# Expert rows of six tiles gathered as quarter rows and turned by VectorE, in a mixture-of-experts layer

## The chip, the cores and the metric

The kernel runs on one core of a Trainium2 chip. The metric is the device time of one execution in microseconds (us); lower is better. The times below are of three runs, and one further execution was recorded by the hardware profiler. The core's engines work side by side and meet at semaphores: TensorE (PE; its weight loads are PEld), VectorE (DVE), ScalarE (ACT), GpSimd (POOL) and SyncE (SP), the last two issuing the DMAs.

## The reference

An attention block and a mixture-of-experts block, each behind a layer norm and with a residual:

```
x: (2, 512, 512) f32
x = x + attention(layernorm(x))            # 32 heads of 16
t = layernorm(x)                           # 1024 tokens x 512
p = softmax(t @ gate_w.T)                  # 8 experts
top_vals, top_idx = top_k(p, 2); top_vals /= sum(top_vals)
h1, h3 = t @ w1[e].T, t @ w3[e].T          # (512 -> 800) for each expert e
y[e] = (silu(h1) * h3) @ w2[e].T           # (800 -> 512)
x = x + sum over the token's 2 experts of top_vals * y[e]
```

All is float32. The kernel computes only the chosen experts. It splits each float32 operand into a rounded part (`_hi`) and a rest (`_lo`) and forms a product from three matmuls in the fast 32-bit type: hi x hi, hi x lo, lo x hi.

## The kernel before

**The stage around the change.** After attention and routing (from about 289 us of the span to its end) eight "tiles" of token rows are worked through, tile i = 0 to 7, each for one expert, in order of how many tokens the experts have. Tile 0 holds 256 rows, tile 1 302, and each further one 12 fewer: 290, 278, 266, 254, 242, 230 (`CAPS`). A tile consists of sub-tiles ("subs") of up to 128 rows: tile 0 has two, tiles 1 to 4 three (the thirds have 46, 34, 22 and 10 rows) and tiles 5 to 7 two. Extra tiles beyond the eighth run in a loop only when an expert has more tokens; here there are none.

**Rows in.** The normed rows lie in DRAM (`xn2_dram`, 512 floats a row, row 0 all zeros). GpSimd gathers a tile's rows with one indirect DMA for each sub, the row numbers coming from `from_row`, into `xg`, which has one buffer of three subs. TensorE turns each sub with four transposes (`rows_in`, L1016) into PSUM, so that the 512 hidden features lie on 128 partitions in four chunks (chunk c holds features c*128 to c*128+127). ScalarE copies the turned rows to `xgT_hi` (`rows_hi`, L1335) and VectorE forms `xgT_lo` (`rows_lo`, L1733).

**A step.** Step i is the work on tile i.
- `up(i)`: seven units (u = 0 to 6) of TensorE products of w1 and w3 with the rows. For each unit ScalarE applies silu (L1316), VectorE multiplies (`gated`, L1750), and both split the product into `act_hi` (L1323) and `act_lo` (`inner_lo`, L1762). The last unit, u=6, is short and stacked: VectorE sums (`tail_sum`, L1740), ScalarE applies silu (L1313), VectorE multiplies (L1754), ScalarE copies twice (L1326, L1327), VectorE writes the last piece of `act_hi` (L1766). That one releases the short matmul that ends a group of the second product ("tail": L1110 by columns, L1133 by rows).
- The second product. Tiles 1 to 4 (three subs) go "by columns": four quarters h = 0 to 3 of the output (`down`), 18 matmuls and a tail each, in two PSUM banks, so quarter h waits until ScalarE has copied out quarter h-2 (`hidden_out`, L1347). The tail of quarter 0 stands late in quarter 1. Tiles 0 and 5 to 7 (two subs) go "by rows" (`down_rows`), one output of 512 columns for each sub.
- In this second part of step i, TensorE also transposes the rows of tile i+1: one sub before each of the quarters 0, 1 and 2 by columns; by rows the first sub before the first output, the second before its tail.
- Behind the last `act_hi`, ScalarE's order is `rows_hi` of sub 0, a split of the next tile's weights (L1263), `hidden_out` of quarter 0, `rows_hi` of sub 1, two splits, `hidden_out` of quarter 1, and so on; VectorE's is `rows_lo` of sub 0, two splits (L1577), `rows_lo` of sub 1, two splits, `rows_lo` of sub 2, the rest.
- `up(i+1)` waits for all `xgT_lo` of tile i+1.

**GpSimd's order** in its loop over i: wait until TensorE has transposed tile i+1 (`s_xt`), gather tile i+2 into `xg`, then add the rows of tile i to the output with indirect DMAs (`add_rows`, L679), each after ScalarE has scaled a sub (`y_out`, L1360, early in step i+1). SyncE loads the weights of tile i+1 (w13 in three pieces, w2) as soon as the splits of tile i's have freed the landing buffers.

The order on every engine is written out by hand; the semaphores `s_xg` (rows landed), `s_xt`, `s_xh`, `s_xl` (turned, hi, lo) count subs.

## Time and profile before

| | us |
|---|---|
| median of 3 runs | 544.2 (543.85 to 544.46) |
| the profiled execution | 544.47 |
| its span in the trace | 542.7 |
| TensorE busy | 528.0 (97%) |
| VectorE busy | 386.5 (71%) |
| ScalarE busy | 321.2 (59%) |
| GpSimd busy | 116.9 (22%) |

The trace gives for each instruction its start and length in us from the span's start, its engine, its line in the kernel and its operands, and the idle time of the engine before it with what ended it. Matmuls are pipelined: one of 0.30 us can be followed by the next 0.13 us later, so the distance of starts is what counts. The chain of waits is the work that ended last, followed back from the end: its pieces add up to the span. For a DMA, the time from issue to landing is listed apart.

### The profile page before, as it was taken

The numbers are of one execution on the slowest core, as the hardware profiler recorded it, in microseconds if no ns is written. First come the engines' busy times: TensorE is split into PE (matmuls) and PEld (weight loads), VectorE is DVE, ScalarE is ACT, GpSimd is POOL, SyncE is SP. The second block draws the span as 40 slices with busy tenths as digits, with TensorE's granted clock in tenths as the row PEclk, the third lists the DMA queues.
The fourth block names the chain that finished last, engine by engine and source line by source line (L and its number), as shares of the span: only waits on it lengthen the run. The fifth ranks groups of instructions, "written<-read, shape, count | busy, mean of one in ns | idle before, by whom it ended". The sixth has DMA issues, their size and how long they took to land.

```text
span 542.7 us, 10567 instructions
## 1 busy us (share of the span) xinstructions
PE 528.0 (97%) x3925; PEld 388.4 (72%) x3925; DVE 386.5 (71%) x722; ACT 321.2 (59%) x476; POOL 116.9 (22%) x146
## 2 busy tenths in 40 slices
PE   7999999999999999999999999999999999999992
PEld 6887665343333434334868989999999999999991
DVE  6924766999998999943979986836648284666650
ACT  4422115888778788777373465746576575757540
POOL 3400111001020220722001320432342321242112
PEclk9999999999999999999999999999999999999997
DMA  8381267675685470033645698774846757585122
GB/s 298 148 104 14 42 110 84 103 95 79 97 104 74 72 159 15 14 101 99 240 159 170 225 372 266 198 259 111 312 80 220 223 154 269 124 297 162 40 36 38
DMA packets 29743, 78.24 MB, mean 144 GB/s; under 512 B 8572, under 2 KB 9596, under 8 KB 25210
## 3 DMA queue, kind: packets, MB, share of 16 engines
q1 hardware_dynamic: 24394, 68.84, 47.1%
q0 software_dynamic: 5296, 8.69, 8.6%
q8 instruction: 33, 0.54, 0.5%
q14 instruction: 20, 0.16, 0.1%
HBM read 53.11 MB, written 9.32 MB: 115 GB/s over the span
## 4 chain that ended last, share of the span: by engine, by line
PE 89%; DVE 5%; DMA 1%; issue 1%; POOL 1%; ACT 1%; SPq 0%; POOLq 0%; DVEq 0%
PE ps L719 17%; PE ps L721 16%; PE ps L720 16%; PE ps_o L734 12%; PE ps L747 7%; PE ps L759 5%; PE ps_m L747 3%; DVE neg_max L1458 3%; PE ps L787 2%; PE ps_o L719 1%; PE ps_m L1016 1%; DMA x_sb<-x 1%; PE ps L1068 1%; PE ps L1071 1%; PE ps_o L720 1%
## 5 line engine op out<-in xcount | busy, mean ns | idle before, releaser
L1241 ACT ACTIVATE probs_t<-ps 128x1024 f32<-128x1024 f32 x128 | 125.7, 1023 | 28.1 <-PE ps_o L734 23.6
L1458 DVE TENSOR_REDUCE neg_max<-ps 128x1 fp32r<-128x512 f32 x171 | 111.2, 681 | 7.2 <-PE ps L747 4.5
L719 PE MATMUL ps<-xgT_hi,w_hi 128*128 128x256 f32 (+7 forms) x380 | 109.4, 288 | 0.0
L721 PE MATMUL ps<-xgT_hi,w_lo 128*128 128x256 f32 (+7 forms) x380 | 108.6, 286 | 0.0
L720 PE MATMUL ps<-xgT_lo,w_hi 128*128 128x256 f32 (+7 forms) x380 | 108.5, 286 | 0.0
L759 PE MATMUL ps<-q_stack,k_stack 49*128 49x512 f32 x256 | 83.8, 444 | 0.0
L734 PE MATMUL ps_o<-probs_t,v_ones 128*32 128x256 f32 (+1 forms) x944 | 79.6, 409 | 0.1
L719 PEld LDWEIGHTS ps<-xgT_hi,w_hi 128*128 128x128 f32 x380 | 72.0, 189 | 0.3 <-DVE xgT_lo L1733 0.2
L720 PEld LDWEIGHTS ps<-xgT_lo,w_hi 128*128 128x128 f32 x380 | 72.0, 190 | 0.1
L721 PEld LDWEIGHTS ps<-xgT_hi,w_lo 128*128 128x128 f32 x380 | 72.0, 189 | 0.0
L747 PE MATMUL ps<-k_stack,q_stack 48*128 48x512 f32 x171 | 68.6, 458 | 0.5 <-DVE neg_max L1458 0.5
L1750 DVE TENSOR_TENSOR act<-gate,ps 128x256 f32<-128x256 f32 (+7 forms) x48 | 20.7, 430 | 65.2 <-PE ps L721 52.9
L1458 DVE TENSOR_REDUCE neg_max<-ps_m 128x1 fp32r<-128x512 f32 x85 | 57.9, 681 | 1.6 <-PE ps L747 1.0
L1577 DVE TENSOR_TENSOR w_lo<-w_sb,w_hi 128x1024 fp32r<-128x1024 f32 x48 | 56.6, 1219 | 0.4 <-ACT w_hi L1263 0.4
L1316 ACT ACTIVATE gate<-ps 128x256 f32<-128x256 f32 (+7 forms) x48 | 18.9, 393 | 61.1 <-PE ps L721 60.6
L747 PEld LDWEIGHTS ps<-k_stack,q_stack 48*128 48x128 f32 x171 | 28.0, 184 | 35.0 <-DVE neg_max L1458 22.6
L734 PEld LDWEIGHTS ps_o<-probs_t,v_ones 128*32 128x32 f32 x944 | 18.6, 107 | 42.7 <-issue 37.3
L1263 ACT ACTIVATE w_hi<-w_sb 128x1024 fp32r<-128x1024 f32 x48 | 48.5, 1056 | 0.2
L747 PE MATMUL ps_m<-k_stack,q_stack 48*128 48x512 f32 x85 | 38.3, 451 | 0.0
L759 PEld LDWEIGHTS ps<-q_stack,k_stack 49*128 49x128 f32 x256 | 32.9, 184 | 7.5 <-ACT probs_t L1241 7.4
L637 POOL TENSOR_TENSOR q_hi<-q_hi,rec_all 128x512 f32<-128x512 f32 x7 | 9.0, 1282 | 125.5 <-DVE rec_all L1551 125.5
L679 POOL DMA_INDIRECT out<-xn,to_now x20 | 33.8, 1691 | 6.2 <-issue 6.2
(326 smaller groups left out, 981.6 us busy)
## 6 DMA issues: line engine op xcount, KB each, us to landing
w_sb<-w SPq DMA_DIRECT2D x16, 1024.0 KB, 7.2
w_sb<-w SPq DMA_DIRECT2D x8, 1536.0 KB
w_sb<-w SPq DMA_DIRECT2D x8, 1152.0 KB, 8.3
q_stack<-q_hi SPq DMA_DIRECT2D x32, 128.0 KB, 4.8
k_stack<-k_hi SPq DMA_DIRECT2D x32, 128.0 KB, 4.6
q_stack<-q_lo SPq DMA_DIRECT2D x16, 128.0 KB, 4.4
k_stack<-k_lo SPq DMA_DIRECT2D x16, 128.0 KB, 5.7
q_hi<-o_raw SPq DMA_DIRECT2D x16, 128.0 KB, 4.8
```

The costliest lines, as they stand in the source:

```text
L679: pool.indirect_dma_start(out=out[:, :], out_offset=bass.IndirectOffsetOnAxis(ap=to_now[0:rows, m:m + 1], axis=0), in_=y_sb[0:rows, m, :], ...
L719: pe.matmul(o, x_hi, w_hi, start=start, stop=False)
L720: pe.matmul(o, x_hi, w_lo, start=False, stop=False)
L721: return pe.matmul(o, x_lo, w_hi, start=False, stop=stop)
L734: last = pe.matmul(ps_o[32 * j:32 * j + 32, q0:q1], v_ones[:, (g // 8) * TPB + kc, (g % 8) * GH + j, :, :].rearrange("p d o -> p (d o)"), ...
L747: pe.matmul(max_bank(g, u2), q[:, qt * P:(qt + 1) * P], k, start=True, stop=True).then_inc(s_sn, 1)
L759: last = pe.matmul(ps4[:, 2 * (n % 2) + c, :], k[:, kc * P:(kc + 1) * P], q, start=True, stop=True)
L1241: a.activation(probs_t[:, kc % 2, 2 * half:2 * half + 2, :], ps4[:, 2 * (n % 2):2 * (n % 2) + 2, :], ACT.Exp, scale=D ** -0.5).then_inc(s_ ...
L1263: a.activation(w13_hi[:, at], w13_sb[:, at], ACT.Copy).then_inc(s_hi13, 1)
L1458: v.tensor_reduce(neg_max[:, g % 2, col:col + 1], max_bank(g, u2), AX.X, ALU.max, negate=True).then_inc(s_mx, 1)
L1577: v.tensor_tensor(w13_lo[:, at], w13_sb[:, at], w13_hi[:, at].bitcast(f32), ALU.subtract).then_inc(s_lo13, 1)
L1750: v.tensor_tensor(act[:, u % 2, 0:cap], gate[:, u % 2, 0:cap], ps4[:, pair + 1, 0:cap], ALU.mult).then_inc(s_act, 1)
```

## The change

Tiles 2 to 7 are no longer transposed by TensorE. Each row of 512 floats is taken as four quarter rows of 128 floats (512 bytes). For a sub, GpSimd issues one gather for each block of 32 rows; a gather fetches 128 quarter rows: partition 32a+j receives quarter a of row 32g+j. VectorE then transposes, in place, blocks of 32x32 in `xg`, of which element k of a block's row lies at step 4 (one instruction for each sub, `pieces_turned`); afterwards partition p holds features 4p to 4p+3 of every row, and ScalarE and VectorE read `xg` where they read PSUM before. The features are therefore dealt to the four chunks in another order, and so are the rows of w1 and w3 (on the host) and the transposes of tiles 0 and 1, which TensorE keeps (`chunk_in`, a step of 4 floats in the stationary operand). The numbers of the quarter rows are computed by sixteen small VectorE operations in step 0 (`pieces_from`). GpSimd waits for `rows_lo` of tile i+1 instead of for TensorE's transposes before it gathers tile i+2.

```diff
+PIECED = 2
+PIECED_AT = SUBS * PIECED
...
+        from_piece = sb(ctx, "from_piece", [P, MORE_AT - PIECED_AT, P // BLOCK], u32)
...
+        def pieced(i):
+            return isinstance(i, int) and i >= PIECED
+        def blocks_of(i, m):
+            return -(-rows_of_sub(i, m) // BLOCK)
...
+        def turned_rows(i, m):
+            if pieced(i):
+                turned = xg[:, m, :].rearrange("p (t c) -> p c t", c=HC)
+            else:
+                turned = rows_bank(i, m).rearrange("p (c t) -> p c t", c=HC)
+            return turned[:, :, 0:rows_of_sub(i, m)]
...
+            def pieces_in(i):
+                pool.tensor_tensor(carrier[:, SUBS + i:SUBS + i + 1], dump_1[:, 0:1], dump_1[:, 0:1], ALU.add)
+                for m in range(subs_of(i)):
+                    for g in range(blocks_of(i, m)):
+                        at = sub_at(i) + m - PIECED_AT
+                        pool.indirect_dma_start(
+                            out=xg[:, m, g * P:(g + 1) * P], out_offset=None,
+                            in_=xn2_dram[:, :].rearrange("r (a k) -> (r a) k", a=P // BLOCK),
+                            in_offset=bass.IndirectOffsetOnAxis(ap=from_piece[:, at, g:g + 1], axis=0)).then_inc(s_piece[m], 16)
...
             for i in range(E):
                 if i < E - 2:
-                    pool.wait_ge(s_xt, subs_ahead(i + 2))
-                    rows_in(i + 2, 2 * i + 2)
+                    if i == 0:
+                        pool.wait_ge(s_from, 1)
+                        pool.wait_ge(s_xt, subs_ahead(2))
+                    else:
+                        pool.wait_ge(s_xl, subs_ahead(i + 2))
+                    pieces_in(i + 2)
...
+            def chunk_in(m, rows, c):
+                return xg[0:rows, m, :].rearrange("r (p c) -> r c p", c=HC)[:, c, :]
...
-                    last = pe.transpose(rows_bank(i, m)[:, c * P:c * P + rows], xg[0:rows, m, c * P:(c + 1) * P],
-                                        ident[0:rows, 0:rows])
+                    last = pe.transpose(rows_bank(i, m)[:, c * P:c * P + rows], chunk_in(m, rows, c), ident[0:rows, 0:rows])
...
-                follows = isinstance(i, int) and i < LAST
+                follows = isinstance(i, int) and i + 1 < PIECED
...
                     for h in range(HC):
-                        if h < subs_of(i + 1):
-                            rows_in(i + 1, h)
                         down(i, h)
...
             def rows_hi(i, m):
-                a.wait_ge(s_xt, subs_ahead(i) + m + 1)
+                if pieced(i):
+                    a.wait_ge(s_xd, subs_pieced(i) + m + 1)
+                else:
+                    a.wait_ge(s_xt, subs_turned(i) + m + 1)
...
+            def pieces_from():
+                for a in range(P // BLOCK):
+                    for g in range(P // BLOCK):
+                        ins = v.tensor_scalar(from_piece[BLOCK * a:BLOCK * (a + 1), :, g],
+                                              inv[BLOCK * g:BLOCK * (g + 1), 0, PIECED_AT:MORE_AT],
+                                              float(P // BLOCK), float(a), ALU.mult, ALU.add)
+                ins.then_inc(s_from, 1)
+            def pieces_turned(i):
+                for m in range(subs_of(i)):
+                    n = blocks_of(i, m)
+                    v.wait_ge(s_piece[m], 16 * (pieces_ahead(i, m) + n))
+                    blocks = xg[:, m, 0:n * P].rearrange("p (g k c) -> p g c k", k=BLOCK, c=HC)
+                    v.transpose(blocks, blocks).then_inc(s_xd, 1)
...
                     if u == NU - 2:
                         inner_lo(i, u, cap)
+                        if opening:
+                            pieces_from()
+                        elif isinstance(i, int) and i < LAST:
+                            pieces_turned(i + 1)
...
-    gate_w, up_w = (w.transpose(0, 2, 1).reshape(E, HC, P, F).transpose(0, 2, 1, 3) for w in (w1, w3))
+    gate_w, up_w = (w.transpose(0, 2, 1).reshape(E, P, HC, F) for w in (w1, w3))
```

## Rows read from the trace of the kernel before

**Rows 1.** The page: busy us and share by engine; the chain by engine.

```profile
PE 528.0 (97%) x3925; PEld 388.4 (72%) x3925; DVE 386.5 (71%) x722; ACT 321.2 (59%) x476; POOL 116.9 (22%) x146
PE 89%; DVE 5%; DMA 1%; issue 1%; POOL 1%; ACT 1%; SPq 0%; POOLq 0%; DVEq 0%
```

**Rows 2.** Chain of waits, second product of step 2: start us, us, what.

```profile
376.81 0.44 PE ps_m L1016 x4
...
382.24 0.14 PE ps L719
382.78 0.35 PE ps_m L1016 x4
383.13 0.33 PE ps L719
```

**Rows 3.** Timeline, VectorE, end of step 2: start, us, engine, line, operation, operands, [idle before].

```profile
376.22 1.06 DVE L1762 TENSOR_TENSOR act_lo<-act,act_hi 128x290 fp32r<-128x290 f32 x2
377.29 0.45 DVE L1740 TENSOR_TENSOR tail_sum<-ps,tail_lo 64x290 f32<-64x290 f32 x1
...
379.67 0.45 DVE L1766 TENSOR_TENSOR act_hi<-act,act_hi 32x290 fp32r<-32x290 f32 x1 [0.97 <-ACT act_hi L1327]
380.30 0.69 DVE L1733 TENSOR_TENSOR xgT_lo<-ps_m,xgT_hi 128x512 fp32r<-128x512 f32 x1 [0.17 <-ACT xgT_hi L1335]
380.90 2.35 DVE L1577 TENSOR_TENSOR w_lo<-w_sb,w_hi 128x1024 fp32r<-128x1024 f32 x2
...
386.12 0.24 DVE L1733 TENSOR_TENSOR xgT_lo<-ps_m,xgT_hi 128x88 fp32r<-128x88 f32 x1
```

**Rows 4.** Timeline, ScalarE, copies of quarters 0 and 1 in steps 1 to 4.

```profile
348.70 0.42 ACT L1347 ACTIVATE x<-ps 128x302 f32<-128x302 f32 x1 [1.06 <-PE ps L1110]
...
382.28 0.41 ACT L1347 ACTIVATE x<-ps 128x290 f32<-128x290 f32 x1 [0.93 <-PE ps L1110]
...
414.63 0.41 ACT L1347 ACTIVATE x<-ps 128x278 f32<-128x278 f32 x1 [0.75 <-PE ps L1110]
...
417.31 0.40 ACT L1347 ACTIVATE x<-ps 128x278 f32<-128x278 f32 x1
...
445.69 0.39 ACT L1347 ACTIVATE x<-ps 128x266 f32<-128x266 f32 x1 [0.47 <-PE ps L1110]
...
448.35 0.39 ACT L1347 ACTIVATE x<-ps 128x266 f32<-128x266 f32 x1
```

**Rows 5.** Timeline, TensorE, first matmul of quarter 3 in steps 3 and 4.

```profile
417.95 0.29 PE L719 MATMUL ps<-act_hi,w_hi 128*128 128x278 f32 x1
...
448.79 0.39 PE L719 MATMUL ps<-act_hi,w_hi 128*128 128x266 f32 x1
```

**Rows 6.** Instructions on the tile `max_rows`: ns min/median/max, first and last start.

```profile
L1468 DVE STREAM_TRANSPOSE max_rows<-neg_max x16: 199/202/213, 67.8 to 235.2; 128x32 f32<-128x32 f32 x16
```

**Rows 7.** Timeline, VectorE, two small independent operations of the routing.

```profile
286.79 0.18 DVE L1631 TENSOR_SCALAR over_at<-first 128x8 f32<-128x8 f32 x1
286.89 0.15 DVE L1632 SCALAR_TENSOR_TENSOR base_e<-place,cap_e 128x8 f32<-128x8 f32 x1
```

**Rows 8.** Timeline, VectorE and TensorE, second product of step 5.

```profile
473.70 0.41 DVE L1766 TENSOR_TENSOR act_hi<-act,act_hi 32x254 fp32r<-32x254 f32 x1 [0.91 <-ACT act_hi L1327]
...
475.16 0.56 PE L1016 MATMUL ps_o<-ident,xn 114*128 114x114 f32 x4
```

**Rows 9.** Timeline, VectorE and TensorE, end of step 0.

```profile
320.17 0.34 DVE L1733 TENSOR_TENSOR xgT_lo<-ps_m,xgT_hi 128x184 fp32r<-128x184 f32 x1
...
320.64 0.33 PE L719 MATMUL ps<-xgT_hi,w_hi 128*128 128x302 f32 x1
```

**Rows 10.** Gathers on GpSimd: one in the timeline; all of L658; from issue to landing.

```profile
385.18 1.86 POOL L658 DMA_INDIRECT xn<-xn_rows,from_now  x1 [0.30 <-issue]
...
L658 POOL DMA_INDIRECT xn<-xn_rows,from_now x18: 901/1049/1930, 300.2 to 478.8; - x18
...
DMA to landing us min/median/max: 3.5/7.0/13.1
```

More of the change, by code:

```diff
@@ L209, in moe_layer @@
         to_now = sb(ctx, "to_now", [P, SUBS], u32)
-        carrier = sb(ctx, "carrier", [P, SUBS + 1])
+        carrier = sb(ctx, "carrier", [P, SUBS + E])
         passed = sb(ctx, "passed", [P, E, E])
@@ L282, in moe_layer @@
         s_xt, s_xh, s_xl = (sem(n) for n in ("s_xt", "s_xh", "s_xl"))
+        s_piece = [sem(f"s_piece{m}") for m in range(SUBS)]
+        s_from, s_xd = sem("s_from"), sem("s_xd")
         s_ug, s_up, s_silu, s_act = (sem(n) for n in ("s_ug", "s_up", "s_silu", "s_act"))
@@ L406, in landed, with pieces_ahead, subs_pieced, subs_turned @@
             return i if m < 2 else thirds(i)
+        def pieced(i):
+            return isinstance(i, int) and i >= PIECED
+        def blocks_of(i, m):
+            return -(-rows_of_sub(i, m) // BLOCK)
+        def pieces_ahead(i, m):
+            return sum(blocks_of(n, m) for n in range(PIECED, i) if m < subs_of(n))
+        def subs_pieced(i):
+            return subs_ahead(i) - subs_ahead(PIECED)
+        def subs_turned(i):
+            return subs_ahead(i) if isinstance(i, int) else subs_ahead(i) - subs_pieced(E)
+        def whole_rows(i, m):
+            return landed(i, m) if isinstance(i, int) else i - (E - PIECED)
+        def turned_rows(i, m):
[4 more added lines that the diff above has]
+            return turned[:, :, 0:rows_of_sub(i, m)]
         def unit_at(u):
@@ L692, in _ @@
             gather(from_row_0, 0)
-            pool.tensor_tensor(carrier[:, SUBS:], dump_1[:, 0:1], dump_1[:, 0:1], ALU.add).then_inc(s_sent, 1)
+            pool.tensor_tensor(carrier[:, SUBS:SUBS + 1], dump_1[:, 0:1], dump_1[:, 0:1], ALU.add).then_inc(s_sent, 1)
             pool.wait_ge(s_where, 2)
@@ L704, in _ @@
                 added(i)
-                add_rows(i, 2 * i + 3 if i < E - 2 else E + i)
+                add_rows(i, i + 2)
             n = tiles_taken(pool)
@@ L708, in _ @@
                 with pool.If(i < n):
-                    rows_in(i, 2 * i)
+                    rows_in(i, 2 * i - (E - 2))
                     added(i)
-                    add_rows(i, 2 * i + 1)
+                    add_rows(i, 2 * i - (E - 3))
                     added(i + 1)
@@ L1005, in slot_weights @@
                 last.then_inc(s_invw, 1)
+            def chunk_in(m, rows, c):
+                return xg[0:rows, m, :].rearrange("r (p c) -> r c p", c=HC)[:, c, :]
             def rows_in(i, m):
                 rows = rows_of_sub(i, m)
-                pe.wait_ge(s_xg[m], 16 * (landed(i, m) + 1))
+                pe.wait_ge(s_xg[m], 16 * (whole_rows(i, m) + 1))
                 if not isinstance(i, int):
@@ L1121, in down_rows @@
                         pe.wait_ge(s_al, NU * i + c + 1)
-                    if m == 1 and c == FC // 2 and isinstance(i, int) and i < LAST and subs_of(i + 1) == SUBS:
+                    if m == 1 and c == FC // 2 and isinstance(i, int) and i == 0:
                         rows_in(i + 1, 2)
@@ L1162, in _ @@
                 for c in range(2):
-                    at = slice((2 * half + c) * P, (2 * half + c + 1) * P)
-                    last = pe.transpose(ps2[:, half, c * P:(c + 1) * P], xg[:, 1, at], ident[:, :])
+                    last = pe.transpose(ps2[:, half, c * P:(c + 1) * P], chunk_in(1, P, 2 * half + c), ident[:, :])
                 last.then_inc(done, 1)
@@ L1334, in rows_hi @@
                 rows = rows_of_sub(i, m)
-                a.activation(xgT_hi[:, :, m * P:m * P + rows],
-                             rows_bank(i, m).rearrange("p (c t) -> p c t", c=HC)[:, :, 0:rows],
-                             ACT.Copy).then_inc(s_xh, 1)
+                a.activation(xgT_hi[:, :, m * P:m * P + rows], turned_rows(i, m), ACT.Copy).then_inc(s_xh, 1)
             def hidden_out(i, h):
@@ L1732, in rows_lo @@
                 at = slice(m * P, m * P + rows)
-                v.tensor_tensor(xgT_lo[:, :, at], rows_bank(i, m).rearrange("p (c t) -> p c t", c=HC)[:, :, 0:rows],
-                                xgT_hi[:, :, at].bitcast(f32), ALU.subtract).then_inc(s_xl, 1)
+                v.tensor_tensor(xgT_lo[:, :, at], turned_rows(i, m), xgT_hi[:, :, at].bitcast(f32),
+                                ALU.subtract).then_inc(s_xl, 1)
+            def pieces_from():
[11 more added lines that the diff above has]
+                    v.transpose(blocks, blocks).then_inc(s_xd, 1)
             def gated(i, u, cap):
```

2 lines of the change are left out of this document (1 added, 1 removed).

## The prediction, made before the changed kernel was run

> **What bounds the kernel now.** I read the page first: TensorE is busy 97% of the span and carries 89% of the chain of waits [rows 1], and in the chain's own order of time the TensorE transposes of the gathered rows stand in it, 0.44 us for a group of four on 128 rows [rows 2]. So removing them looks like a plain gain. The timelines of VectorE and ScalarE around one tile's end say more. I call "step i" the work on tile i; the change touches steps 1 to 6, where tiles 2 to 7 are turned. In step 2, VectorE comes to `tail_sum` (L1740) with no idle time before it, straight from `act_lo` [rows 3]; from there a chain of single operations runs between VectorE and ScalarE (sum, silu, product, two copies, the last `act_hi` at 379.67, then ScalarE's `xgT_hi`, a weight split, and the `hidden_out` copy at 382.28) [rows 3, 4]. The reader is to see two things: whatever is put ahead of L1740 shifts this whole chain, and `hidden_out` of the first quarter (called h0) waited only 0.93 us for TensorE. TensorE cannot start its third quarter before it. In step 4 the copy of the second quarter at 448.35 is followed at 448.79 by TensorE's first matmul of the fourth quarter [rows 4, 5]: there this chain already is what ends last.
>
> **The change, part by part.** The sum is made against the profiled execution, 544.47 us (span 542.7); it lies 0.3 us above the median of 544.2.
>
> (1) TensorE's transposes removed. Fifteen sub-tiles of four transposes: twelve of full or nearly full rows at about 0.44 us, three short thirds (34, 22 and 10 rows) at 0.35 us [rows 2]. 12 x 0.43 + 3 x 0.35 = 6.2 us. The third is followed by an L719 of 0.33 instead of the usual 0.13 us, most of which is the wait for `hidden_out` and stays. Alone this would be -6.2 us.
>
> (2) VectorE's block transposes, placed after `act_lo` of u=5 and ahead of L1740. The only transpose in the trace has 32 elements a partition and takes 202 ns [rows 6]. A 512-element `xgT_lo` (L1733) occupies VectorE 0.61 us from its start to the next start (380.30 to 380.90) [rows 3]; I take 0.61 us for a full sub-tile, 0.34 for 256 elements and 0.21 for 128. So the delay D is 1.56 us in step 1 (two subs and two blocks), 1.43 in steps 2 and 3, 1.22 in steps 4 to 6. The ends: the 202 ns of the row may be nearly all start-up, so 0.3 us for a full sub is possible; and since the blocks are read and written in place at a step of four elements, twice the price (1.15 us) is too. I take 0.61 because it is one element per 1.04 ns as in every other 32-bit VectorE row here.
>
> The Trainium skill, Vector Engine (DVE) Microarchitecture Reference, section 3.8, says the transposing array is pipelined to sustain one element per cycle per lane; by it the sum would be the one below. SBUF — State Buffer, section Door 1, says the memory is read in 16-byte lines and that an access which crosses to a new line pays a penalty, while it calls a step of four fp32 free; a step of four fp32 is a new line each time, so the first half of that rule speaks against this change. No row here shows a data operand read so; it belongs to rival B.
>
> What D does in the column steps (1 to 4): h0's copy moves by D less its idle time, less 0.1 us by which consecutive ScalarE operations overlap. Idle times are 1.06, 0.93, 0.75 and 0.47 us [rows 4], so it moves by +0.4, +0.4, +0.6 and +0.6 us. The second quarter's copy follows the first by fixed ScalarE work (one `xgT_hi`, two splits): 2.68 us in step 3, 2.66 in step 4 [rows 4], against 19 matmuls of 0.13 us in a quarter [rows 2], so it moves by the same. TensorE's fourth quarter can start 0.44 us after that copy starts (step 4). In step 3 it started at 417.95, 0.64 us after it: 0.2 us of room [rows 4, 5]; to steps 1 and 2, where the copy moves less, I charge 0 and 0.1. The loss is therefore 0, 0.1, 0.4 and 0.6 us, and 0.1 us per restart of TensorE in steps 1 to 3: +1.4 us in all, with the whole 4.5 us that TensorE saves there spent waiting for `hidden_out`. The new tile's `xgT_lo` is complete at 386.12 + 0.24 + 1.43 = 387.8 [rows 3], still ahead of tile 3's first matmul, which can come no earlier than 382.28 + 0.4 + 2.68 + 0.44 + 2.5 = 388.3, so nothing more is late.
>
> (3) Steps 5 and 6, tiles by rows. TensorE's tail (L1133) needs the last `act_hi`, which VectorE ends at 473.70 + 0.41; with D it ends at 475.33. Without transposes TensorE is there at 475.16 - 0.44 = 474.7; before, at 475.16 + 0.35 = 475.5 [rows 8]. So the gain is 0.1 us in step 5 and by the same reading 0.2 us in step 6: -0.4 us with the dearer matmul after each removed group.
>
> (4) `pieces_from`: sixteen small VectorE operations on 32 x 19 elements, in step 0, again ahead of L1740. Two small independent operations follow each other by 0.10 us [rows 7]: 1.6 us; at their full duration (0.17) 2.7. In step 0 tile 1 still goes through TensorE, and its last `xgT_lo` ends at 320.51, 0.13 us before TensorE begins tile 1 at 320.64 [rows 9]. Nothing covers it: +1.5 us.
>
> (5) The pieces on GpSimd. Tiles 2 to 7 issue 10, 9, 9, 8, 8 and 8 gathers instead of 15 in all; each occupies the queue about 1.05 + 0.3 us by the median, 1.86 + 0.3 in the row of step 2 that has the weight loads beside it [rows 10]. I take 1.55. Tile 4's gathers can begin when tile 3's `xgT_lo` has been read, 386.4; 9 x 1.55 + 0.5 = 14.5 us, and landing takes 3.5 to 13.1, median 7.0 us [rows 10]: 408. They are wanted one step after 377.29; a step is 32.3 us (382.28 to 414.63) [rows 4], so 409.6. The later tiles have shorter steps and 8 gathers (1.6 us less). It is covered, by 1 to 2 us. Behind them GpSimd's scatter of the tile before goes some 4 us later; its next reader comes 15 us after. Nothing is moved past SyncE's queue: its loads wait for the splits of the tile before, which move by D, and are read a stage later. The bytes are the same, the descriptors more.
>
> (6) Tiles 0 and 1 load the stationary rows at a step of four elements. No row prices it: zero to double (+0.14 us for each of 12 in the path, 1.7 us). I take zero, the time of the dense row. ScalarE's and VectorE's reads of turned rows from SBUF instead of PSUM: VectorE pays the same for an element of `w_lo` (2 x 1024, both operands in SBUF, 2.35 us) and of `xgT_lo` (one in PSUM) [rows 3]; for ScalarE I allow +0.03 us twice in four steps, +0.2. Reordered weights cost nothing: same shapes, and host work.
>
> Sum: +1.4 - 0.4 + 1.5 + 0.2 = +2.7 us, 547.2 in the profiled execution, 547.0 as a median.
>
> **Rivals.**
> A, the cover holds (faster). Place: VectorE's slot ahead of L1740. If a full sub costs 0.3 us, D is 0.6 to 0.8 us, the column steps gain 1.5 and the row steps 1.6 us: 544.2 + 1.5 - 3.1 + 0.2 = 542.8. If it does not shift the chain at all, 544.2 - 6.2 + 1.5 = 539.5. It decides from about 0.4 us per sub downwards. For it: VectorE is idle 29% of the span [rows 1], and a 202 ns row says little on slope. Against: no idle before L1740 [rows 3]. 0.20.
> B, strides cost double. D grows by 4.8 us over steps 1 to 4 and 2.1 over 5 and 6: 547.0 + 6.9 = 553.9; with ScalarE's reads at double too (+0.4 us, twice in four steps) 557. 0.15.
> C, pieces come late. With 2.2 us per gather and the median landing, tile 4 lands 0.5 + 19.8 + 7 = 27.3 us after 386.4, 4 us after it is wanted, and VectorE waits with gated(6), hence TensorE, behind it: 1 to 5 us in each of six steps, 15 us: 562. It decides from 1.65 us per gather. For: the row of 1.86 us [rows 10]. Against: the median of 18 is 1.05. 0.12.
> D, nothing: the parts cancel within 1.1 us (a small `pieces_from`, D nearer 0.5 per sub): 544.2. 0.11.
> My forecast, 545.3 to 550: 0.42.
>
> **How the numbers follow.** What a measurement can tell from no change is 0.2%, 1.1 us. Faster 0.20 (A), same 0.11 (D), slower 0.42 + 0.15 + 0.12 = 0.69. The range 541.5 to 557 leaves out the far end of A (0.08) and most of C (0.11). The likeliest case's own range is 545.3 to 550.
>
> **What would show it.** No L1016 in steps 1 to 6, but TensorE idle before its third quarter, about 1 us in each of steps 1 to 4, released by ScalarE's L1347; a STREAM_TRANSPOSE of 512 elements about 0.7 us long, three or two per step, with no idle before it (idle there, released by the gather's DMA, is C; 1.1 us or more is B; 0.4 is A); L1740 later behind the last L1762 by D; sixteen small operations in step 0 and tile 1 begun 1.5 us later. The forecast is wrong if `hidden_out` is not what TensorE waits for.

## The result, and the profile after

| | before | after |
|---|---|---|
| median, us | 544.12 (6 runs, 543.7 to 544.57) | 562.01 (6 runs, 561.9 to 562.25) |
| ratio | | 1.0326, 95% interval 1.0315 to 1.0337 |
| span of the profiled execution | 542.7 | 560.5 |

The change makes the kernel 3.3% slower. I had forecast 547.0, with a range up to 557. The sign was right, the size was not, and no case of the prediction gives 562 for the reason that the traces show.

The table holds the distance from the first product of one tile to that of the next, read off the timelines of TensorE; "end" runs from the first product of tile 7's second part to the end of the span. It shows where the time went, and the same reading of the experiments (told of below) stands beside it.

| us | before | after | no_turn | dense_blocks | apart_and_early |
|---|---|---|---|---|---|
| step 0 | 29.25 | 33.58 | 32.08 | 32.11 | 29.49 |
| step 1 | 34.29 | 37.06 | 33.95 | 35.28 | 33.92 |
| step 2 | 33.34 | 35.33 | 33.26 | 34.51 | 32.54 |
| step 3 | 32.14 | 34.46 | 32.26 | 33.59 | 31.50 |
| step 4 | 30.85 | 33.22 | 31.34 | 33.08 | 30.47 |
| step 5 | 28.96 | 29.80 | 28.12 | 29.01 | 28.10 |
| step 6 | 26.81 | 27.73 | 25.99 | 26.96 | 26.05 |
| first part of tile 7 | 16.95 | 17.06 | 16.95 | 17.05 | 16.95 |
| end | 18.74 | 20.71 | 20.72 | 20.74 | 20.67 |

Four places lose: step 0 (4.3 us), the column steps 1 to 4 (9.5 us), the row steps 5 and 6 (1.8 us), and the end (2.0 us), which the prediction did not have at all.

The page of after, to be laid beside [rows 1]: busy time by engine, the chain by engine, and the granted clock in 40 slices.

```profile
PE 528.6 (94%) x3865; PEld 385.6 (69%) x3865; DVE 406.3 (72%) x753; ACT 327.1 (58%) x476; POOL 172.6 (31%) x177
PE 74%; DVE 12%; ACT 5%; issue 4%; DMA 1%; POOL 1%; SPq 0%; ACTq 0%; DVEq 0%; POOLq 0%
PEclk9999999999999999999999899899999999999996
```

TensorE's share of the chain fell from 89% to 74%; VectorE's rose from 5% to 12% and ScalarE's from 1% to 5%. TensorE's busy time is as large as before although 60 transposes are gone: a matmul at half the clock counts twice (in no_turn below, where the clock does not fall, it is 524.8).

VectorE at the end of step 2, against [rows 3] (timeline: start, us, engine, line, operation, operands, idle time before).

```profile
383.51 1.06 DVE L1832 TENSOR_TENSOR act_lo<-act,act_hi 128x290 fp32r<-128x290 f32 x2
384.49 2.37 DVE L1804 STREAM_TRANSPOSE xn<-xn 128x512 f32<-128x512 f32 x3
386.75 0.41 DVE L1810 TENSOR_TENSOR tail_sum<-ps,tail_lo 64x290 f32<-64x290 f32 x1
...
389.10 0.45 DVE L1836 TENSOR_TENSOR act_hi<-act,act_hi 32x290 fp32r<-32x290 f32 x1 [0.97 <-ACT act_hi L1379]
390.23 1.09 DVE L1786 TENSOR_TENSOR xgT_lo<-xn,xgT_hi 128x512 fp32r<-128x512 f32 x1 [0.68 <-ACT xgT_hi L1390]
```

The transposes have no idle time before them, so the pieces were there. From the start of the two `act_lo` to that of `tail_sum` there are now 3.24 us (386.75 - 383.51), before 1.07 (377.29 - 376.22): D is 2.17 us where I had taken 1.43. And `xgT_lo`, which now reads the turned rows at a step of 4, takes 1.09 us in place of 0.69.

ScalarE in the same place, against [rows 4].

```profile
389.09 1.11 ACT L1390 ACTIVATE xgT_hi<-xn 128x512 fp32r<-128x512 f32 x1
390.11 1.04 ACT L1315 ACTIVATE w_hi<-w_sb 128x1024 fp32r<-128x1024 f32 x1
391.17 0.41 ACT L1400 ACTIVATE x<-ps 128x290 f32<-128x290 f32 x1
391.48 1.14 ACT L1390 ACTIVATE xgT_hi<-xn 128x512 fp32r<-128x512 f32 x1
392.51 2.01 ACT L1315 ACTIVATE w_hi<-w_sb 128x1024 fp32r<-128x1024 f32 x2
394.41 0.41 ACT L1400 ACTIVATE x<-ps 128x290 f32<-128x290 f32 x1
```

The two copies of quarters (L1400) lie 3.24 us apart; in [rows 4] they lay 2.68 apart in step 3. The difference is one `xgT_hi` at 1.1 us where one from PSUM took 0.6. Neither copy has idle time before it: ScalarE's own queue sets their times.

What TensorE waited for there (its idle time stands in brackets), and its waits over the whole span (total, times, longest).

```profile
389.60 0.40 PE L1165 MATMUL ps<-act_hi,w_hi 96*128 96x290 f32 x1 [1.08 <-DVE act_hi L1836]
391.64 0.40 PE L771 MATMUL ps<-act_hi,w_hi 128*128 128x290 f32 x1 [1.09 <-ACT x L1400]
394.87 0.40 PE L771 MATMUL ps<-act_hi,w_hi 128*128 128x290 f32 x1 [0.41 <-ACT x L1400]
```

```profile
PE ps L771 <- ACT x L1400: 5.9, 7, 1.2
PE ps L1165 <- DVE act_hi L1836: 4.8, 4, 1.3
PE ps L1188 <- DVE act_hi L1836: 4.6, 3, 2.2
```

The second of these rows is the tail of quarter 0, released by the last `act_hi`: a pause of TensorE ahead of the one for `hidden_out` (L1400), which I had not looked for. It is not on the chain that ended last. That chain (start us, us, what) passes it by, through ScalarE:

```profile
389.09 0.97 ACT xgT_hi L1390
...
391.48 1.14 ACT xgT_hi L1390
392.62 1.90 ACT w_hi L1315 x2
394.52 0.31 ACT x L1400
394.87 0.40 PE ps L771
```

In steps 1 to 4 alike, ScalarE comes to its copies of quarters 0 and 1 with no idle time, so by this reading a shorter pause at the tail would only make the one behind it longer; no run took it away alone.

The end of step 0, against [rows 9]: the sixteen small operations, and TensorE's tail behind them.

```profile
312.29 2.97 DVE L1793 TENSOR_SCALAR from_piece<-inv 32x17 uint32<-32x17 f32 x16
315.30 0.42 DVE L1810 TENSOR_TENSOR tail_sum<-ps,tail_lo 64x256 f32<-64x256 f32 x1
```

```profile
317.99 0.50 PE L1188 MATMUL ps<-w_hi,act_hi 96*128 96x512 f32 x1 [2.18 <-DVE act_hi L1836]
318.33 0.43 PE L771 MATMUL ps<-w_hi,act_hi 128*128 128x512 f32 x1
318.56 0.62 PE L772 MATMUL ps<-w_lo,act_hi 128*128 128x512 f32 x1
318.98 0.63 PE L773 MATMUL ps<-w_hi,act_lo 128*128 128x512 f32 x1
```

TensorE paused for 2.18 us; half a microsecond later its matmuls of 512 columns follow each other at 0.43 us instead of 0.23. The busy time by window shows why: the granted clock (the column after POOL's) is near 0.5, the 1.2 GHz level, for 3.4 us, and a second time in step 1, there behind pauses of 1.13 and 1.07 us.

```profile
318.40:321.80 3.40, 3.40 (x10) 2.43 (x8) 3.00 (x4) 3.17 (x4) 0.00 (x0) 0.52 1.06 331
356.00:359.00 3.00, 3.00 (x14) 3.00 (x13) 3.00 (x4) 3.00 (x6) 0.00 (x0) 0.52 0.35 70
```

In the trace of before the clock is at its full level from 4 us of the span until the last product has ended. A fall does not follow each such pause. In the trace of a later run of the same kernel (after_again, told of below) the same matmul waits as long,

```profile
318.85 0.50 PE L1188 MATMUL ps<-w_hi,act_hi 96*128 96x512 f32 x1 [2.19 <-DVE act_hi L1836]
```

and the clock stays at its full level; step 0 takes 32.09 us there against 33.58, so this fall costs 1.5 us. Last, the prices (ns min/median/max over the trace) and the gathers of the pieces, against [rows 6, 7, 10].

```profile
L1804 DVE STREAM_TRANSPOSE xn<-xn x15: 385/1093/1133, 347.8 to 514.3; 128x512 f32<-128x512 f32 x12, 128x128 f32<-128x128 f32 x2, 128x256 f32<-128x256 f32 x1
...
L1793 DVE TENSOR_SCALAR from_piece<-inv x16: 165/173/179, 312.3 to 315.1; 32x17 uint32<-32x17 f32 x16
...
L713 POOL DMA_INDIRECT xn<-xn_rows,from_piece x52: 944/952/2497, 323.6 to 506.9; - x52
...
DMA to landing us min/median/max: 2.6/3.1/4.8
```

The pieces land in 3.1 us, not 7.0, and a gather occupies GpSimd for 0.95 us. Rival C's figure was 562 and so is the result, but its mechanism is absent: no VectorE instruction waited for a piece.

### The profile page after: what moved, and what is told of

The parts are those of the page before. It is cut to its first block, busy times and chain, and to the rows that moved or that the text cites. A ratio compares the mean times of both kernels' runs of the same rounds, so it can differ in the third digit from the quotient of the medians.

```text
span 560.5 us, 10495 instructions
## 1 busy us (share of the span) xinstructions
PE 528.6 (94%) x3865; PEld 385.6 (69%) x3865; DVE 406.3 (72%) x753; ACT 327.1 (58%) x476; POOL 172.6 (31%) x177
## 4 chain that ended last, share of the span: by engine, by line
PE 74%; DVE 12%; ACT 5%; issue 4%; DMA 1%; POOL 1%; SPq 0%; ACTq 0%; DVEq 0%; POOLq 0%
PE ps L771 14%; PE ps L773 13%; PE ps L772 13%; PE ps_o L786 10%; PE ps L799 6%; PE ps L811 5%; DVE neg_max L1511 5%; PE ps_m L799 3%; PE ps L839 2%; ACT xgT_hi L1390 2%; DVE xn L1804 1%; ACT w_hi L1315 1%; PE ps_o L771 1%; DMA x_sb<-x 1%; DVE w_lo L1630 1%
## 5 line engine op out<-in xcount | busy, mean ns | idle before, releaser
L713 POOL DMA_INDIRECT xn<-xn_rows,from_piece x52 | 55.3, 1064 | 15.0 <-issue 13.7
L727 POOL DMA_INDIRECT out<-xn,to_now x20 | 36.8, 1838 | 4.4 <-issue 3.8
```

What stands on the lines that cost most here:

```text
L713: pool.indirect_dma_start(out=xg[:, m, g * P:(g + 1) * P], out_offset=None, in_=xn2_dram[:, :].rearrange("r (a k) -> (r a) k", a=P // BLOC ...
L727: pool.indirect_dma_start(out=out[:, :], out_offset=bass.IndirectOffsetOnAxis(ap=to_now[0:rows, m:m + 1], axis=0), in_=y_sb[0:rows, m, :], ...
```

## The experiments

Ratios are to the kernel before, timed beside them on the same chip (544.3 to 544.8 us). The experiments ran in four groups, each on a chip of its own: 1 to 4; 5, 6, 7 and 10; 8 with half_turned; and the last three of 9. The kernel before moves by at most 0.5 us from one to the other; times of experiments of different groups are compared with that in mind.

**1. No transposes (no_turn).** VectorE's transposes are left out; ScalarE waits for the pieces themselves.

```diff
-                    a.wait_ge(s_xd, subs_pieced(i) + m + 1)
+                    a.wait_ge(s_piece[m], 16 * (pieces_ahead(i, m) + blocks_of(i, m)))
...
-                        elif isinstance(i, int) and i < LAST:
-                            pieces_turned(i + 1)
```

> The changed kernel with VectorE's block transposes left out (ScalarE waits for the pieces themselves; the rows are read unturned, so the result is not the reference's). Theory (VectorE's 2.0 to 2.6 us a step, put ahead of tail_sum, push the chain to hidden_out): steps 1 to 4, which together are 9.5 us longer than before, come to about before (slow reads of xg at a step of 4 still cost: -0.5 to +0.5 us), steps 5 and 6 gain 3.4 us: about 548.5 us, 547 to 551. Rival (the pieces or GpSimd's 52 gathers are what disturbs): nothing moves much, above 558.

547.96 us (547.64 to 549.05), ratio 1.0069 (1.0052 to 1.0085). As the theory said. So the transposes cost 14.0 us, and the rest of the change is not a gain either: 3.6 us slower than before, of which step 0 has 2.8 and the end 2.0; steps 1 to 6 together are 1.5 us shorter than before, all of it in steps 5 and 6. Steps 1 to 4 are 0.2 us longer than before, and TensorE still waits there for `hidden_out`. In the trace the clock did not fall, although the pause of 2.18 us in step 0 is there too.

**2. The small operations on GpSimd (from_on_gpsimd).**

```diff
...
-                        if opening:
-                            pieces_from()
-                        elif isinstance(i, int) and i < LAST:
+                        if not opening and isinstance(i, int) and i < LAST:
                             pieces_turned(i + 1)
```

GpSimd runs the sixteen, one after the other, behind its gathers of tile 1.

> The changed kernel with the sixteen operations of pieces_from on GpSimd, idle at that time, instead of on VectorE. Theory (they stand in the chain at 0.18 us each, 3.0 us, and the wait of TensorE that they cause is followed by 3.4 us at the lower granted clock, some 1.5 us more): step 0 comes back from +4.3 to about 0 us: 557.8 us. Rival (only the 3.0 us themselves are lost, the clock falls anyway): 559.0 us.

559.52 us (557.67 to 559.85), ratio 1.0278 (1.0261 to 1.0295). The median is the rival's: what is gained is the operations, 2.5 us. The profiled execution is the fastest, 557.67, and there step 0 is back at 29.56 us: 2.5 us for the operations (against the 32.08 of no_turn) and 1.5 us for a fall of the clock that after has in its trace and this one has not. The other three took 559.4 to 559.9 us, with a mean granted clock of 0.979 to 0.983 against 0.988: they had more time at the lower clock, where in the span is open.

**3. Turned rows written densely (dense_turned).** The transposes read at a step of 4 and write side by side into buffers of their own; ScalarE and VectorE then read without a step.

```diff
...
                     blocks = xg[:, m, 0:n * P].rearrange("p (g k c) -> p g c k", k=BLOCK, c=HC)
-                    v.transpose(blocks, blocks).then_inc(s_xd, 1)
+                    to = turned_to(m)[:, 0:n * P].rearrange("p (g c j) -> p g c j", g=n, c=HC)
+                    v.transpose(to, blocks).then_inc(s_xd, 1)
```

> The changed kernel, its transposes writing dense into a second buffer (read at a step of 4 elements, written at a step of 1), so that ScalarE and VectorE read the turned rows in runs of 32. Theory a (every access at a step of 4 costs double, and a transpose that reads so is slow whatever it writes): transposes stay at 1.09 us, xgT_hi falls from 1.12 to 0.6 us and xgT_lo from 1.09 to 0.69; the two xgT_hi ahead of the copies give back 0.9 us in each of steps 1 to 4: 558.4 us. Theory b (the strided write is what costs): the transposes fall to 0.7 us too, another 5 us: 553 us. Rival (SBUF instead of PSUM is the price of the reads, not the step): xgT_hi stays at 1.1 us, 562.

559.5 us (558.77 to 560.0), ratio 1.0279 (1.0262 to 1.0296). The groups by shape (busy us, mean ns) of this kernel and of after:

```profile
L1817 DVE STREAM_TRANSPOSE xn<-xn 128x512 f32<-128x512 f32 x12 | 12.4, 1071 | 0.0
...
L1400 ACT ACTIVATE xgT_hi<-xn 128x512 fp32r<-128x512 f32 x12 | 7.5, 625 | 0.1
```

```profile
L1390 ACT ACTIVATE xgT_hi<-xn 128x512 fp32r<-128x512 f32 x9 | 10.1, 1127 | 0.1
```

ScalarE's copy falls from 1.13 to 0.63 us and is still read from SBUF: the step of 4 was its price, not the memory. The transpose stays at 1.07 with a dense output: a strided read alone is enough for the full price. The median is 2.5 us lower. In its trace the clock falls in steps 1 and 4, in that of after in steps 0 and 1; in steps 2 and 3, where neither has a fall, the dense copies give back 0.85 and 0.91 us, in steps 5 and 6 0.25 and 0.22.

**4. Transposes earlier (early_turn).** In VectorE's idle time behind units 1 to 3, not ahead of `tail_sum`; the pieces still go through the one buffer.

```diff
+                    if 1 <= u <= 3 and not opening and isinstance(i, int) and i < LAST and u - 1 < subs_of(i + 1):
+                        pieces_turned(i + 1, [u - 1])
...
-                        elif isinstance(i, int) and i < LAST:
-                            pieces_turned(i + 1)
```

> The changed kernel with the transposes of sub m placed behind unit u = m+1 of the products, where VectorE waits 2.3 to 4 us for TensorE, instead of all behind u=5. Theory (place, not amount, is the cost): the same as with the transposes left out, 548.5 us, 547 to 551, as long as the pieces have landed by then (first sub some 3 us after its fourth gather). Rival (any VectorE time in a step is paid for): above 556.

556.9 us (555.08 to 560.01), ratio 1.0231 (1.0214 to 1.0248): in the rival's range, but for a reason that the theory had named as its condition. VectorE now waits for the pieces (VectorE's waits; the profiled execution is the slowest of the five):

```profile
DVE xn L1804 <- DMA xn<-xn_rows,from_piece: 26.9, 12, 6.3
```

GpSimd may gather tile i+2 only when tile i+1's `xgT_lo` is read, so the pieces come in time for the late place and not for the early one. This is rival C's mechanism, made by moving the reader.

**5. TensorE kept busy (kept_warm).** Dummy products ahead of the waited tails of steps 0 and 1.

```diff
+                        if isinstance(i, int) and i == 1:
+                            pe.wait_ge(s_act, NU * i + NU - 2)
+                            keep_warm(ps4[:, 1, :], 14)
...
+                    if isinstance(i, int) and i == 0:
+                        pe.wait_ge(s_act, NU * i + NU - 2)
+                        keep_warm(ps4[:, 1, :], 22)
```

> After, with dummy products of TensorE into a free bank ahead of the waited tail in steps 0 and 1 (22 and 14 of them), so that TensorE does not stand there; nothing else changes, the wait itself stays as long. Theory (the fall of the granted clock to 0.5 for 3.4 us is called by the pause of 2.2 us and of 1 us that the changed kernel makes ahead of those tails, and costs half of its length, 1.7 us each time): both falls are gone, steps 0 and 1 are 1.7 us shorter each, 558.7 us in all, if no fall comes elsewhere in their place. Rival (the clock falls for a reason other than the pause): both falls stay and the time is 562 or more.

562.04 us (559.18 to 562.66), ratio 1.0311 (1.0281 to 1.0342). In its trace both falls are gone, step 0 takes 32.10 us in place of 33.58 and step 1 36.26 in place of 37.06; but step 4, where nothing was added, now has a fall of 6.8 us, begun between pauses of 1.26 and 1.16 us, and takes 35.10 in place of 33.22. The median has not moved. That the dummy products kept the clock up is not shown by this trace: in step 0 the same pause of 2.2 us has no fall behind it in the traces of no_turn, dense_turned, dense_blocks and after_again either. In step 1 the evidence is a little better: the four traces with transposes of the full price in that place (after, after_again, from_on_gpsimd, dense_turned) all have a fall there, and this one has none. What the traces do show together: the five in which TensorE never pauses for more than 0.6 us in this stage (before, those of experiments 6, 7 and 8, and apart_and_early) have no fall in it, and of the ten with such pauses nine have one to five. A fall of 3.4 us cost 0.7 to 1.5 us of its step (after_again against after, in steps 4 and 0), the one of 6.8 us 1.9.

**6. Strided stationary operand alone (strided_stationary).** The kernel before, with `chunk_in`'s access for all tiles.

```diff
-                    last = pe.transpose(rows_bank(i, m)[:, c * P:c * P + rows], xg[0:rows, m, c * P:(c + 1) * P],
-                                        ident[0:rows, 0:rows])
+                    last = pe.transpose(rows_bank(i, m)[:, c * P:c * P + rows],
+                                        xg[0:rows, m, :].rearrange("r (p c) -> r c p", c=HC)[:, c, :], ident[0:rows, 0:rows])
...
```

> The kernel before, with only the order of the features dealt anew: all tiles are transposed by TensorE as before, but from a stationary operand of which the elements lie at a step of 4 floats. Each weight load then takes 0.21 us in place of 0.14 (the loads in the changed kernel show that), 76 of them in the stage. Theory (a transpose waits for its weight load, so each is 0.07 later): 544.3 + 76 x 0.07 = 549.6 us at most, and at least half of that since most lie in the second product: 547 to 549.6. Rival (the load lies beside the product ahead of it, as the forecast had it): within 544.3 and 545.3.

545.87 us (545.41 to 546.48), ratio 1.0035 (1.0021 to 1.0049): between the two. A weight load takes 0.21 us in place of 0.14, but only 1.5 us of 76 x 0.07 = 5.3 reach the end. The change has 16 such loads at this line in place of 76, so its share is below the 1.7 us that I had as the far end; step 0 has 0.3 us of it (29.56 against 29.25 there and in from_on_gpsimd).

**7. Five more semaphores (five_semaphores)** in the kernel before, used by nothing.

```diff
+        more = [sem(f"more{m}") for m in range(5)]
```

> The kernel before with five more semaphores that nothing uses, as many as the change adds. Theory (the 2 us that every kernel with the change has longer behind its last scatter are spent on clearing or handing over more semaphores): 546.3 us, and 8.7 us from the end of the last scatter on GpSimd to the end of the span in place of 6.8. Rival (the 2 us come from the scatters or the code itself): 544.3 and 6.8 us.

544.39 us, ratio 1.0003 (0.9994 to 1.0013). The theory falls: the 2 us at the end are not theirs.

**8. More gathers (more_gathers).** The kernel before with 36 further indirect DMAs.

```diff
+                    for n in range(6 * i, 6 * i + 6):
+                        pool.indirect_dma_start(
+                            out=more[:, n, :], out_offset=None, in_=xn2_dram[:, :].rearrange("r (a k) -> (r a) k", k=8),
+                            in_offset=bass.IndirectOffsetOnAxis(ap=from_row_0[:, 0:1], axis=0)).then_inc(s_more, 16)
...
```

> The kernel before, with 36 further gathers on GpSimd (8 floats a row into a buffer that nothing reads, 6 behind each tile's own), so that it issues nearly as many indirect DMAs as the changed kernel. GpSimd's last instruction, the drain of its queue, takes 3.4 us in the kernel before and 6.7 in each kernel with the pieces. Theory (the drain grows with the number of indirect DMAs that were issued): the drain takes 6 us or more and the time is 546 to 546.5. Rival (it grows with the code or with something else of the change): 3.4 us and 544.3, up to 545 if the added gathers hold up the scatters.

546.71 us (546.1 to 547.25), ratio 1.0032 (1.0021 to 1.0043), 1.9 us more. The drain that ends GpSimd's program is in the trace's records with 3.43 us in the kernel before (40 indirect DMAs in its trace), 6.28 here (76), 6.72 in after (77). The drain is as long in from_on_gpsimd (6.71 us), where GpSimd has 17 more instructions that are no DMAs, so it goes with the number of indirect DMAs. In after it is 3.3 us longer than before and begins 1.3 us sooner behind the last scatter, which leaves the 2.0 us at the end. In the trace of more_gathers 1.5 us are added at the end and 0.5 in step 0: most of the 2 us is shown, 0.5 is open.

**9. Half of the blocks, and dense blocks (half_turned, then dense_blocks, half_again and after_again together).** A price near the forecast's 0.61 us can be had in two ways: half as many strided blocks (the first edit), or as many blocks whose elements lie side by side (the second).

```diff
-                    blocks = xg[:, m, 0:n * P].rearrange("p (g k c) -> p g c k", k=BLOCK, c=HC)
+                    blocks = xg[:, m, 0:(n + 1) // 2 * P].rearrange("p (g k c) -> p g c k", k=BLOCK, c=HC)
```

```diff
-                    blocks = xg[:, m, 0:n * P].rearrange("p (g k c) -> p g c k", k=BLOCK, c=HC)
+                    blocks = xg[:, m, 0:n * P].rearrange("p (n k) -> p n k", k=BLOCK)
```

> After, with only half of each sub's blocks transposed by VectorE (2 of 4, 1 of 2), so that an instruction takes some 0.55 us in place of 1.09, which is near the 0.61 that the forecast took; the rest of the rows stays unturned, so this kernel leaves part of the computation out. Without any transposes the time was 548.0, with all 562.0. Theory (the place and the wait behind it were costed right, and the price of one instruction was not): the transposes cost in a straight line, half of 14.0, so 555.0, 553 to 556.5. Rival (most of the 14 us come past a point: the clock that falls behind longer pauses of TensorE, and ScalarE's copies that are absorbed until then): 550.5 or less.

579.25 us (577.8 to 582.31), ratio 1.0617: neither. In its trace the clock fell five times within the stage, three of them for 6.8 us, and the first parts of steps 2, 3, 4 and 6 (the products of w1 and w3, in which nothing was changed) were 3 to 7 us longer than in after. Hence the repetition on another chip, with the changed kernel as a control:

> After, with VectorE's transposes of the same number and size and at the same place, but of blocks whose elements lie side by side (no step of 4, read and written); the features come out in the wrong order, so this kernel computes something else. Theory (the step of 4 elements is what makes an instruction take 1.09 us; without it it takes 0.55 to 0.65, which the forecast took; place and wait were costed right): 548.0 without transposes plus 6 to 8, so 554 to 556.5. Rival 1 (the instruction takes 1 us or more for another reason, its 512 columns of 4 bytes): 562. Rival 2 (half the price costs less than half, since it is absorbed up to a point): 551 or less.

> The kernel of half_turned once more (half of each sub's blocks transposed, the rest left out of the computation), beside the changed kernel itself and the one with dense blocks. It had taken 579.3, and its products of w1 and w3 in steps 2, 3, 4 and 6 were 4 to 6 us longer each, with pauses of TensorE that nothing in the trace releases and falls of the granted clock of 6.8 us. If that belongs to the chip of that run (a lower limit on TensorE's work there): 551 to 556.5 here. If it belongs to the kernel: again 575 or more.

> The changed kernel itself, as the control of the other two on the same chip: 562.0, with two falls of the granted clock of 3.4 us. If the chip differs in how readily it lowers the clock, this one shows it: other than two falls, and another time with them, while the kernel before stays at 544.3.

dense_blocks 555.32 us (554.47 to 556.66), ratio 1.0203 (1.0185 to 1.0222); half_again 554.96 (554.34 to 555.75), ratio 1.0199 (1.0182 to 1.0216); after_again 562.05 (560.65 to 563.17), ratio 1.0316 (1.0298 to 1.0333). The price of an instruction in dense_blocks, then in half_again:

```profile
L1804 DVE STREAM_TRANSPOSE xn<-xn x15: 268/670/708, 346.2 to 507.7; 128x512 f32<-128x512 f32 x12, 128x128 f32<-128x128 f32 x2, 128x256 f32<-128x256 f32 x1
```

```profile
L1804 DVE STREAM_TRANSPOSE xn<-xn x15: 391/637/668, 346.4 to 506.7; 128x256 f32<-128x256 f32 x12, 128x128 f32<-128x128 f32 x3
```

512 elements at a step of 1 take 0.67 us, at a step of 4 1.09. Near the price that the forecast took, 0.61, both kernels stand at 555. A straight line from 548.0 (no transposes) to 562 (1.09 us) gives 556.6 and 556.1 at their lengths: the time follows the length of these instructions nearly so, with no threshold that would absorb half of them. The control was to show two falls of the clock and has three in the stage in its trace, in steps 1, 3 and 4, and none in step 0; its median is that of after all the same. Why the first run of the half kernel took 579 on its chip is open; the same kernel did not do it on the other chip, and the changed kernel was not timed beside it there.

**10. All of it mended (apart_and_early).** Dense turned rows in buffers of their own (a further small one for the third sub), transposes behind units 1 to 3 (3 to 5 in step 1), the small operations on GpSimd, and GpSimd's wait moved so that the pieces come early:

```diff
-                        pool.wait_ge(s_xl, subs_ahead(i + 2))
+                        pool.wait_ge(s_xd, subs_pieced(i + 2))
```

> The change with three differences: VectorE's transposes write densely into buffers of their own (read at a step of 4, written without one), so that ScalarE and VectorE read without a step and GpSimd may gather the next tile's pieces as soon as those of this one are transposed; the transposes stand behind units u = 1 to 3 of the step (3 to 5 in step 1) in place of ahead of tail_sum; the sixteen small operations are GpSimd's. Theory: transposes left out gave 548.0; without the small operations in step 0 this falls by 2.5 (29.56 against 32.08 for step 0), without the strided reads of xgT_hi and xgT_lo by about 2.5 (562.0 against 559.5), and the transposes cost 0 to 2.5 in VectorE's idle time: 543.0 to 545.5. Rival (the pieces are late for the earlier place as in the run with early transposes alone, or the transposes push `gated` and with it TensorE in every step): 550 or more.

543.12 us (542.35 to 544.23, 10 runs), ratio 0.9981 (0.9971 to 0.9991). It is 19 us faster than the changed kernel and 0.19% faster than the one before, which lies within the 0.2% that the prediction named as its limit for telling a difference. The transposes are as dear as ever (mean 1.10 us) and now cost nothing that can be seen (timeline of VectorE, step 2):

```profile
363.60 0.46 DVE L1854 TENSOR_TENSOR act_lo<-act,act_hi 128x290 fp32r<-128x290 f32 x1
363.97 1.10 DVE L1826 STREAM_TRANSPOSE xn<-xn 128x512 f32<-128x512 f32 x1
366.49 0.46 DVE L1842 TENSOR_TENSOR act<-gate,ps 128x290 f32<-128x290 f32 x1 [1.42 <-PE ps L795]
```

Behind the transpose VectorE still idles 1.42 us for TensorE, and the time is what no_turn gives without the small operations and the strided copies (548.0 - 2.5 - 2.5 = 543.0). Four things were changed together; which of them was needed for it was not tried one by one. Of TensorE's waits for the other engines in the stage 0.9 us are left. Steps 1 to 6 are 3.8 us shorter than before, and 1.9 of that is given back by the drain at the end.

## Why the prediction was wrong, by its own steps

"(1) TensorE's transposes removed ... -6.2 us" alone. With everything around them hidden, apart_and_early gains 3.8 us in steps 1 to 6. The remaining 2.4 us include 0.9 us in which TensorE's matmuls wait for `hidden_out`; the rest was not separated. That TensorE would lose all it saved before its third quarter, released by ScalarE's L1347 (L1400 now), was right.

"(2) VectorE's block transposes ... I take 0.61 us for a full sub-tile." This is the step that failed, and it failed at the choice between the ends, 0.3 and 1.15: the measured 1.09 is the far end. I chose by a row on dense operands, and named in the same breath what made the operand different, a step of 4 elements. (The reason given for 0.61 is wrong too: 0.61 us for 512 elements is 1.19 ns an element, not 1.04.) The condition "1.1 us or more is B" was met, with a mean of 1.10 us. At 0.67 us the whole would have been 555.3 instead of 562.0 (dense_blocks), in the range, but still 8 us above the forecast: the rest lies in (4), (6), the drain and the clock.

The chain behind the transposes was costed right. Steps 2 and 3 can be compared, since none of the traces of after, dense_turned, dense_blocks and half_again has a fall of the clock in them. In after they are together 4.3 us longer than before. Of that the price of the transposes has 1.7 to 1.8 (after less dense_blocks or half_again) and the strided copies 1.8 (after less dense_turned); what is left, 0.7 to 0.9, is what the sum had for these two steps, 0.8 (0.1 and 0.4, two restarts at 0.1, ScalarE's 0.1). The pause at the tail of quarter 0 (4.8 us in after) was not in the prediction and needed no term, since it does not stand on the chain that ended last.

The Trainium skill, SBUF — State Buffer, section Door 1, was the rule to follow: it calls an access that crosses to a new 16-byte line slower, although it calls a step of four fp32 free. The traces agree with the first half alone: a step of 4 floats took VectorE 1.09 against 0.67 us, ScalarE 1.13 against 0.63, and TensorE's weight load 0.21 against 0.14.

"(3) Steps 5 and 6: -0.4." Near the forecast's price they are +0.2 (dense_blocks) or 0.0 (half_again), of which 0.5 belongs to the strided copies; at the true one +1.8. The mechanism, D against the room ahead of the tail, was right, and the size followed from (2).

"(4) Sixteen small operations ... by 0.10 us: +1.5." They follow each other by 0.18 us, near their own duration, which I had as the far end (2.7); from_on_gpsimd puts them at 2.5 us. The pair in [rows 7] worked on 8 elements a partition and on other kinds of operand; what sets the spacing was not tried. That nothing covers them was right.

"(5) It is covered, by 1 to 2 us." Right, and by more: the pieces land in 3.1 us. What the gathers cost is elsewhere, 2.0 us at the final drain (1.5 of it repeated by more_gathers), which no step had.

"(6) I take zero" for the strided stationary operand: 0.3 us in step 0. "+0.2" for ScalarE's and VectorE's reads: this is the second term that was mis-sized. The step of 4 makes it 2.5 us by the medians (dense_turned), 0.9 us in each column step that no fall disturbs. I had the doubling only in rival B.

Not in the prediction at all: the clock. In the profiled execution the pause of 2.18 us in step 0 is followed by 3.4 us at 1.2 GHz, 1.5 us of loss, and the fall in step 1 costs about 1 (the step is 0.8 us longer than in kept_warm, and 2.0 longer than in half_again, of which 0.9 is the price of the transposes, as in the steps next to it).

The sum again, with measured terms, against the 15.1 us that the profiled execution lies above the forecast (17.8 - 2.7). Transposes at 1.09 us instead of one near the forecast's price: 0.9 in each of steps 1 to 4 and 1.7 in steps 5 and 6, 5.3 (after less half_again; step 1, where after has its fall, taken like its neighbours). Strided copies: 0.9 in each of steps 1 to 4 and 0.5 in steps 5 and 6, less the 0.2 that the forecast had, 3.9 (after less dense_turned; steps 1 and 4, where dense_turned has falls, taken like their neighbours). Small operations, 1.0 more. The strided stationary operand in step 0, 0.3. The falls in steps 0 and 1, 1.5 and 1.0. The drain, 2.0. The start and tile 7's first part, 0.3. That is 15.3. It is an account of one execution: in others the falls lie in other steps (after_again), and the median is the same.

Rival B had this mechanism with a chance of 0.15. Its figures for the column and row steps, 9.6 (1.4 + 0.2 + 4.8 + 3.2) and 1.7 us (2.1 - 0.4), stand beside the measured 9.5 and 1.8, of which the fall in step 1 has 1.0. What takes its 557 to 562 is what no case had or had too small: the drain, the small operations, and the fall in step 0 (2.0 + 1.0 + 1.5).

## What to carry to other kernels

Price an operand by its step as well as by its size: here a step of 4 floats cost TensorE's weight load, VectorE and ScalarE half as much again to nearly double (0.14 to 0.21, 0.67 to 1.09, 0.63 to 1.13 us), and a buffer written densely by one engine frees all its readers of it. Work for an idle engine pays only in the slot where it idles, and moving it there needs its data earlier, that is another buffer and a weaker wait for the producer. Where the bounding engine pauses at several places of one chain, the pauses do not add up: find which one the chain that ended last goes through. And before two traces are subtracted, look at the granted clock in each stretch of both: a fall in the one and not in the other passes for a cost of the change.

## What the runs showed of the hardware

- GpSimd's final drain grows with the number of indirect DMAs issued in the whole kernel: 3.43 us after 40, 6.28 after 76, 6.72 after 77; 36 added ones cost 1.9 us of the total, 1.5 of it at the end of the trace.
- TensorE's granted clock fell to half for 3.4 or 6.8 us in a stage in which TensorE paused for 1 to 2.7 us and was otherwise dense, not behind each such pause and not in the same steps in each execution: behind the pause of 2.2 us in step 0 it fell in four traces (after, half_again, early_turn, and half_turned with 2.7) and in four it did not. Without a pause over 0.6 us in the stage it did not fall in it (five traces).
- A 32x32-block transpose of 128x512 floats takes VectorE 0.67 us dense, 1.07 to 1.09 with a strided read, whether or not the output is strided. A strided output with a dense read was not tried.
- Gathers of 128 pieces of 512 bytes landed in 3.1 us (2.6 to 4.8); those of whole rows of 2 KB [rows 10] in 7.0 (3.5 to 13.1).
